# Inverse square roots: ten VectorE operations replaced by one elementwise power on GpSimd

## The chip, the cores and the metric

The kernel runs on one core of a Trainium2 chip. The metric is device time in microseconds (us), the median of several runs. The core has five engines that work side by side and meet only at semaphores: TensorE (PE, matrix products, with its weight loads as PEld), VectorE (DVE), ScalarE (ACT), GpSimd (POOL) and SyncE (SP, which issues DMAs). GpSimd has done little here: it fills constants, copies a few tiles and shares one solve with VectorE.

## The reference

One decoder layer over 16 sequences of 128 tokens with 128 channels (4 heads of 32), all float32: a delta-rule attention with gates, a cross attention without softmax, a feed-forward layer with 8 experts of which the best 2 count, and a layer norm behind each. Inverse roots and roots stand in four places of it:

```python
def l2norm(x):
    return x * jax.lax.rsqrt(jnp.sum(x * x, -1, keepdims=True) + 1e-06)      # of q and k, per head

def head_stats(x):
    mean = x.mean(-1)
    var = ((x - mean[..., None]) ** 2).mean(-1)
    am = jnp.abs(x).mean(-1)
    l2 = jnp.sqrt((x * x).sum(-1))
    return jnp.stack([mean, var, am, l2], -1).mean(2)      # mean over the heads

def rmsnorm(x, w):
    return x * jax.lax.rsqrt((x * x).mean(-1, keepdims=True) + EPS) * w

x = _layernorm(x + attention(x))
x = _layernorm(x + cross_attention(x, ctx))
x = _layernorm(x + experts(x))
```

head_stats is taken of four sources (short filter, long filter, delta-rule output, v) and of their gated mixture.

## The kernel before

The 16 sequences are worked in NG = 4 groups of G = 4. Each engine has one instruction list, written out by hand in program order, and nothing reorders it; engines wait for one another by counting semaphores. The stages, in order of time:

1. Projections (to about 110 us). Per group TensorE projects four sequences (line 460), ScalarE applies SiLU (L876) and squares q and k (L882), and VectorE in `norms` sums the squares per head (L1175), adds 1e-6 (L1178), takes the inverse root of 32 numbers per partition and scales k (L1182) and k times beta (L1189). TensorE transposes these keys (`keys_transposed`, L442) only after the next group's first projection; ScalarE copies them (L902, L906), and then the products L493 run. For the last group there is no next projection to stand in between.
2. Triangular inverse (124 to 160 us). VectorE (L1430, L1432) and GpSimd (L409, L413) share it; its input and output go through DRAM. Around it VectorE makes the statistics of v (k = 3), of the short filter (k = 0) and, later, of the long filter (k = 1): `source_sums`, then `source_moments`, each on 64 numbers per partition.
3. The delta rule (174 to 226 us): a chain of small matrix products (L721, L733, L757) on TensorE. Behind it `source_moments(2, 0, G)` finishes the statistics of the delta output for group 0 (16 numbers per partition), GpSimd copies them (`stats_of`, L425), and TensorE transposes them (L576).
4. Gates, cross attention and experts (235 us to the end). Group 0 first goes through the gate alone: `mixture_stats` (statistics of the mixture, 16 numbers), `gated` (rmsnorm, 16 numbers), `x1_norm` (layer norm, 4 numbers per partition). Then `step(g)` for g = 1, 2, 3 lays three groups over one another: the gate of group g, the cross attention and first experts of p = g - 1, the last experts of q = g - 2. VectorE's order in a step is: add(q, 5), rotate_queries(p), decay_scores(p), source_logits(g), add(q, 6), x2_norm(p), add(q, 7), source_weights(g), route_max(p), mixture(g), choose(p), finish(q), mixture_stats(g), start_sum(p), add(p, 0), add(p, 1), rotate_keys(g), add(p, 2), gated(g), add(p, 3), x1_norm(g), add(p, 4). TensorE's order is fixed in the same way: x1t(p), queries, scores, attend(p), the rest of q's experts, x2t(p), route(p), then experts of p, with st2_transposed(g), output_gate(g), output_z(g), ont(g) and wo(g) among them. A last stretch has the remaining experts of group 3 and its final layer norm.

`rsqrt` (L1140 to L1144) is a guess on the bits and three Newton rounds of three operations. Each operation ends with `own`, which makes VectorE wait for its own result. `layernorm` (x1_norm, x2_norm, finish), `norms`, `head_moments` and `gated` call it. In `head_moments` one more operation ahead (L1257, a floor of 1e-30) and one behind (L1259, times the sum of squares) turn the inverse root into a root.

```python
own(dve.tensor_scalar(y.bitcast(I32), a.bitcast(I32), -0.5, RSQRT_GUESS, ALU.mult, ALU.add))
for i in range(3):
    own(dve.tensor_tensor(out=t, in0=y, in1=y, op=ALU.mult))
    own(dve.scalar_tensor_tensor(out=t, in0=t, scalar=-0.5, in1=a, op0=ALU.mult, op1=ALU.mult))
    own(dve.scalar_tensor_tensor(out=y, in0=t, scalar=1.5, in1=y, op0=ALU.add, op1=ALU.mult))
```

## Time and profile before

| | before |
|---|---|
| median of 3 runs | 512.89 us (512.64 to 513.82) |
| span of the profiled execution, first to last instruction | 510.6 us |
| TensorE busy | 401.5 us (79%), 2952 products |
| VectorE busy | 323.2 us (63%), 1050 instructions |
| ScalarE busy | 159.2 us (31%) |
| GpSimd busy | 39.3 us (8%), 77 instructions |
| mean granted TensorE clock | 0.843 of full speed |

The profiled execution has no device time of its own beside the span; the median of the runs is 2.3 us above the span. Busy time is a sum over stages with different limits, so the table alone does not say what a shorter VectorE is worth. TensorE's clock has two levels, full (1.00, 2.4 GHz) and half (0.50, 1.2 GHz).

### The profile page before, as it was taken

The page shows a single profiled execution, that of the slowest core. Times are in us where ns is not written, and L with a number is a line of the kernel's source. Part 1 is how long each engine was busy: PE and PEld are TensorE (multiplying, and loading weights), DVE is VectorE, ACT ScalarE, POOL GpSimd, SP SyncE. Part 2 cuts the span into 40 slices and gives each one's busy share as a digit, 9 for nine tenths or more (in the row PEclk, how much of TensorE's full clock was granted, in tenths as well). Part 3 has the DMA queues.
Part 4 walks back from the last instruction along what each step waited for, and adds up shares of the span by engine and source line. Part 5 has one row for each costly group of instructions (what it writes and reads, how often), then busy time and mean ns, then how long its engine had stood idle before and what let it go on. Part 6 is the DMA issues. An engine that isn't in the chain of part 4 may idle for free.

```text
span 510.6 us, 8321 instructions
## 1 busy us (share of the span) xinstructions
PE 401.5 (79%) x2952; PEld 293.4 (57%) x2952; DVE 323.2 (63%) x1050; ACT 159.2 (31%) x267; POOL 39.3 (8%) x77
## 2 busy tenths in 40 slices
PE   1979999788973699984245689897998979887992
PEld 0647677467962699971023355565656546564672
DVE  2043464677999823368763576676897588777635
ACT  1252523512345211142021124422433244413430
POOL 7000000002980000000000000000000000000000
PEclk9989999997997555575555969999899989999997
DMA  7460201039653900000000000000020000000000
GB/s 246 105 186 1 42 0 22 1 75 296 166 145 88 119 3 3 3 2 0 1 1 27 15 21 1 0 22 0 2 62 2 21 0 21 0 0 1 22 2 21
DMA packets 48305, 22.23 MB, mean 44 GB/s; under 512 B 17768, under 2 KB 47632, under 8 KB 48016
## 3 DMA queue, kind: packets, MB, share of 16 engines
q1 hardware_dynamic: 31760, 13.40, 10.9%
q10 hardware_dynamic: 16512, 8.39, 6.0%
q8 instruction: 21, 0.34, 0.3%
q14 instruction: 12, 0.10, 0.1%
HBM read 18.64 MB, written 3.15 MB: 43 GB/s over the span
## 4 chain that ended last, share of the span: by engine, by line
PE 49%; DVE 31%; issue 9%; DMA 5%; ACT 3%; SPq 2%; DVEq 0%; ACTq 0%; POOL 0%
PE bank L460 9%; PE bank L493 5%; PE bank L691 5%; PE bank L699 5%; PE bank L721 5%; PE bank L733 4%; PE bank L442 4%; DVE prod L1430 3%; DVE inv L1432 3%; DVE as_t L1410 2%; DVE as_t L1232 2%; DVE nt L1143 2%; DVE nt L1142 2%; DVE as_t L1223 2%; DVE sm L1144 2%
## 5 line engine op out<-in xcount | busy, mean ns | idle before, releaser
L699 PEld LDWEIGHTS bank<-w_sb,as_t 128*128 128x128 f32 x512 | 61.0, 194 | 23.0 <-issue 18.8
L699 PE MATMUL bank<-w_sb,as_t 128*128 128x128 f32 x512 | 63.9, 280 | 5.0 <-ACT as_t L1002 5.0
L1002 ACT ACTIVATE as_t<-bank,cb 128x512 f32<-128x512 f32 x64 | 43.4, 687 | 76.0 <-PE bank L691 60.8
L691 PE MATMUL bank<-as_t,w_sb 128*128 128x512 f32 x128 | 66.5, 648 | 0.0
L1410 DVE SCALAR_TENSOR_TENSOR as_t<-bank,as_t 128x128 f32<-128x128 f32 x128 | 36.0, 344 | 23.4 <-PE bank L699 21.1
L460 PE MATMUL bank<-wtap,xc_pad 128*128 128x384 f32 x128 | 47.0, 514 | 3.8 <-DVE wtap L1157 3.8
L721 PE MATMUL bank<-vb,early 32*32 32x32 f32 x512 | 29.9, 236 | 11.7 <-DMA early<-inverses 11.7
L442 PE MATMUL bank<-ident,as_t 128*128 128x128 f32 (+1 forms) x64 | 12.1, 319 | 33.8 <-DVE as_t L1232 15.7
L1201 DVE TENSOR_TENSOR as_t<-bank,masks 128x512 f32 (+1 forms) x32 | 21.3, 690 | 26.7 <-PE bank L493 26.7
L460 PEld LDWEIGHTS bank<-wtap,xc_pad 128*128 128x128 f32 x128 | 25.0, 202 | 20.3 <-issue 4.3
L721 PEld LDWEIGHTS bank<-vb,early 32*32 32x32 f32 x512 | 28.2, 151 | 13.1 <-issue 12.3
L691 PEld LDWEIGHTS bank<-as_t,w_sb 128*128 128x128 f32 x128 | 24.1, 207 | 20.2 <-issue 18.8
L493 PE MATMUL bank<-early 128*128 128x256 f32 x128 | 31.1, 399 | 2.3 <-ACT early L906 2.3
L442 PEld LDWEIGHTS bank<-ident,as_t 128*128 128x128 f32 (+1 forms) x64 | 7.4, 145 | 42.0 <-DVE as_t L1232 17.3
L493 PEld LDWEIGHTS bank<-early 128*128 128x128 f32 x128 | 25.0, 200 | 5.9 <-ACT early L906 2.5
L442 PE MATMUL bank<-ident,early 128*128 128x128 f32 x96 | 15.8, 295 | 14.8 <-POOL ident L380 7.0
L1447 DVE TENSOR_TENSOR vb<-vb,bank 32x512 f32<-32x512 f32 x12 | 8.2, 686 | 27.0 <-PE bank L733 27.0
L1057 ACT ACTIVATE early<-bank 32x512 f32<-32x512 f32 x16 | 9.4, 588 | 44.3 <-PE bank L721 44.3
L733 PE MATMUL bank<-early,as_t 32*32 32x32 f32 (+2 forms) x384 | 22.7, 239 | 0.0
L442 PEld LDWEIGHTS bank<-ident,early 128*128 128x128 f32 x96 | 11.3, 150 | 18.7 <-POOL ident L380 7.0
L733 PEld LDWEIGHTS bank<-early,as_t 32*32 32x32 f32 (+2 forms) x384 | 21.3, 153 | 0.5
L876 ACT ACTIVATE early<-bank 128x384 f32<-128x384 f32 x16 | 7.9, 491 | 36.4 <-PE bank L462 36.1
(221 smaller groups left out, 647.5 us busy)
## 6 DMA issues: line engine op xcount, KB each, us to landing
toep<-taps_long ACTq DMA_DIRECT2D x8, 1024.0 KB, 7.0
toep<-x SPq DMA_DIRECT2D x8, 256.0 KB, 2.8
early<-x SPq DMA_DIRECT2D x4, 256.0 KB, 4.6
w_sb<-w SPq DMA_DIRECT2D x1, 1024.0 KB
w_sb<-w SPq DMA_DIRECT2D x2, 512.0 KB
blocks<-as_t SPq DMA_DIRECT2D x16, 64.0 KB, 2.0
early<-blocks SPq DMA_DIRECT2D x1, 1024.0 KB, 4.9
toep<-ctx_in SPq DMA_DIRECT2D x4, 256.0 KB, 3.4
```

Of the source, the lines that this page charges most:

```text
L442: last = pe.transpose(ps[dst][0:rows, b * L:(b + 1) * L], source[:, b, :], ident[:, :])
L460: pe.matmul(pr[:, 0:NQKV], xc_pad[:, b, first:first + L], wtap[:, k, :], start=(k == 0), stop=(k == TAPS - 1))
L493: last = pe.matmul(ps[4 + h][:, (b % 2) * 2 * L:(b % 2 + 1) * 2 * L], kh_c[:, h, b, :], kq_c[:, b, :, :].rearrange("p k t -> p (k t)"), st ...
L691: pe.matmul(ps[4 + half][:, :], w1_sb[:, e, half * 128:half * 128 + 128], x2_c.rearrange("p b t -> p (b t)"), start=True, stop=True).then_ ...
L699: last = pe.matmul(bank(6 + e % 2)[:, b, :], hid[:, e % 2, half, b * L:(b + 1) * L], w2_sb[:, e, half, :], start=(half == 0), stop=(half = ...
L721: last = pe.matmul(ps[6 + at % 2][rows, r * DH:(r + 1) * DH], inv_t[rows, GP * g + r, :], vb[rows, GP * g + r, :], start=True, stop=True)
L733: last = pe.matmul(ps[4 + m % 2][rows, r * DH:(r + 1) * DH], as_t[0:CH * n, GP * g + r, 0, rows], u[0:CH * n, GP * g + r, :], start=True, ...
L1002: act.activation(hid[:, e % 2, half, :], ps[4 + half][:, :], ACT.Relu, bias=c_of("b1", 2 * e + half)).then_inc(s["hid_ready"], 1)
L1201: dve.tensor_tensor(out=rows_of[:, bass.ds(g * G + 2 * r, 2), h, :], in0=bank(4 + h, 2), in1=mid(masks[:, :, :].rearrange("p k t -> p (k t ...
L1410: last = dve.scalar_tensor_tensor(out=acc[:, b, :], in0=bank(6 + e % 2)[:, b, :], scalar=score[:, b, e:e + 1], in1=acc[:, b, :], op0=ALU.m ...
L1430: own(dve.tensor_tensor(out=p, in0=blk[:, :, j, j + 1:].unsqueeze(2).broadcast_to([128, 2, m, n]), in1=wide(inv[:, :, 0:m, j], n), op=ALU. ...
L1432: own(dve.tensor_tensor(out=inv[:, :, 0:m, j + 1:], in0=inv[:, :, 0:m, j + 1:], in1=p, op=ALU.subtract))
```

## The change

Every call of `rsqrt` is taken out of VectorE. GpSimd gets a tile `exponents` (64 columns of -0.5, 64 of 0.5) and, for each root, one `tensor_tensor` with the operation `pow`: inverse root for q/k norms, gated rmsnorm and layer norms, root itself for the statistics (so L1257 and L1259 go too). For each of seven kinds there are two semaphores: VectorE raises `<kind>_squares` when the input stands, and waits for `<kind>_roots`. In `head_moments` the signal goes out ahead of the three other moment operations, which VectorE does meanwhile; in the other places VectorE waits at once. GpSimd's list of roots is written in VectorE's order; its loop over the statistics copies is unrolled and split into `source_stats` and `value_stats`, so that the copies stand between the roots.

```diff
+            def root(kind, count, y, a, n, which=0):
+
+                pool.wait_ge(s[kind + "_squares"], count)
+                pool.tensor_tensor(out=y, in0=a, in1=exponents[:, which, 0:n], op=ALU.pow
+                                   ).then_inc(s[kind + "_roots"], 1)
...
             with pool.Fori(0, NG) as g:
                 pool.wait_ge(s["silu_ready"], (g + 1) * G)
                 pool.tensor_copy(src[:, bass.ds(g * G, G), 3, :], qkv_g[:, :, 2 * D:3 * D]).then_inc(s["v_kept"], 1)
+                root("qk", g + 1, rn_g[:, :, :].rearrange("p b h -> p (b h)"),
+                     ss_g[:, :, :].rearrange("p b h -> p (b h)"), G * 2 * H)
+            root("source", 1, sm2[:, :], sumq[:, :], NP, 1)
...
+            for g in range(NG + 1):
+                if g:
+                    root("x2", g, sm2[:, 0:G], sm1[:, 0:G], G)
+                if g >= 2:
+                    root("fin", g - 1, sm2[:, 0:G], sm1[:, 0:G], G)
+                if g == NG:
+                    root("fin", g, sm2[:, 0:G], sm1[:, 0:G], G)
+                    continue
+                root("mixed", g + 1, sm2[:, 0:GP], sumq[:, 0:GP], GP, 1)
+                if g == 0:
+                    root("source", 5, sm2[:, GP:NP], sumq[:, GP:NP], NP - GP, 1)
+                    pool.wait_ge(s["stats_ready"], 5)
+                if g < NG - 1:
+                    source_stats(g + 1)
+                root("gated", g + 1, sm2[:, 0:GP], ogr.rearrange("p b h -> p (b h)"), GP)
+                if g < NG - 1:
+                    value_stats(g + 1)
+                root("x1", g + 1, sm2[:, 0:G], sm1[:, 0:G], G)
...
+            def rooted(kind, count, squares):
+
+                squares.then_inc(s[kind + "_squares"], 1)
+                dve.wait_ge(s[kind + "_roots"], count)
...
-            def head_moments(to, n, first=0):
+            def head_moments(to, n, kind, count, first=0):
 
                 mine = slice(first * H, (first + n) * H)
+                dve.sem_inc(s[kind + "_squares"], 1)
                 own(dve.tensor_tensor(out=sm1[:, mine], in0=sumx[:, mine], in1=sumx[:, mine], op=ALU.mult))
                 own(dve.scalar_tensor_tensor(out=sm1[:, mine], in0=sumq[:, mine], scalar=float(DH),
                                              in1=sm1[:, mine], op0=ALU.mult, op1=ALU.subtract))
-                dve.tensor_reduce(out=to(1), in_=sm1[:, mine].rearrange("p (n h) -> p n h", h=H),
-                                  axis=AX.X, op=ALU.add)
-                own(dve.tensor_scalar(sm2[:, mine], sumq[:, mine], 1e-30, None, ALU.max))
-                rsqrt(nt2[:, mine], sm2[:, mine], n * H)
-                own(dve.tensor_tensor(out=sm2[:, mine], in0=sumq[:, mine], in1=nt2[:, mine], op=ALU.mult))
+                own(dve.tensor_reduce(out=to(1), in_=sm1[:, mine].rearrange("p (n h) -> p n h", h=H),
+                                      axis=AX.X, op=ALU.add))
+                dve.wait_ge(s[kind + "_roots"], count)
                 own(dve.tensor_reduce(out=to(3), in_=sm2[:, mine].rearrange("p (n h) -> p n h", h=H),
                                       axis=AX.X, op=ALU.add))
```

On VectorE, at the last layer norm of the program, there stood before (as_t is the tile that holds the rows and their mean and variance, sm the variance and its inverse root, nt a scratch tile):

```order
L1227 BN_AGGR as_t<-as_t 128x2 x4
L1229 TENSOR_SCALAR sm<-as_t 128x4
L1140 TENSOR_SCALAR sm<-sm 128x4
L1142 TENSOR_TENSOR nt<-sm 128x4
L1143 SCALAR_TENSOR_TENSOR nt<-nt,sm 128x4
L1144 SCALAR_TENSOR_TENSOR sm<-nt,sm 128x4
...
L1232 TENSOR_SCALAR as_t<-as_t,sm 128x128 x4
```

and now:

```order
L1253 BN_STATS as_t<-as_t 128x6 x4
L1257 BN_AGGR as_t<-as_t 128x2 x4
L1259 TENSOR_SCALAR sm<-as_t 128x4
L1261 TENSOR_SCALAR as_t<-as_t,sm 128x128 x4
```

The ten operations are gone; the wait for GpSimd stands between the last two rows. On GpSimd, behind the solve, there stood two fills and then the copies of the statistics in a loop:

```order
L418 MEMSET as_t 128x128
L419 MEMSET as_t 128x128
L425 COPY as_t<-st_all 128x4x16
L427 COPY as_t<-st_all 128x4x4
L432 UNCONDITIONAL_BRANCH
```

and now, from the same two fills to the roots of step 1 (the rows of L401 are the powers):

```order
L433 MEMSET as_t 128x128
L434 MEMSET as_t 128x128
L401 TENSOR_TENSOR sm<-sumq,exponents 128x16
L442 COPY as_t<-st_all 128x4x16
L447 COPY as_t<-st_all 128x4x4
L401 TENSOR_TENSOR sm<-sumq,exponents 128x16
L401 TENSOR_TENSOR sm<-sumq,exponents 128x48
L442 COPY as_t<-st_all 128x4x16
L401 TENSOR_TENSOR sm<-as_t,exponents 128x16
L447 COPY as_t<-st_all 128x4x4
L401 TENSOR_TENSOR sm<-sm,exponents 128x4 x2
L401 TENSOR_TENSOR sm<-sumq,exponents 128x16
```

The powers have 4, 16 or 48 columns there (32 in the projections, 64 around the solve), and each copy now stands behind the power ahead of it.

## Rows read from the trace of the kernel before

**Rows 1.** The page, part 2: TensorE's granted clock in 40 slices

```profile
PEclk9989999997997555575555969999899989999997
```

**Rows 2.** The page, part 4: the chain that ended last, by engine

```profile
PE 49%; DVE 31%; issue 9%; DMA 5%; ACT 3%; SPq 2%; DVEq 0%; ACTq 0%; POOL 0%
```

**Rows 3.** Timeline, x1 norm of group 2: start us, us, engine, line, operation, out<-in

```profile
391.94 0.17 DVE L1140 TENSOR_SCALAR sm<-sm 128x4 int32<-128x4 int32 x1
...
393.92 1.12 DVE L1232 TENSOR_SCALAR as_t<-as_t,sm 128x128 f32<-128x128 f32 x4
```

**Rows 4.** Timeline, moments of the delta output, group 0, and what follows

```profile
231.16 0.17 DVE L1252 TENSOR_TENSOR sm<-sumx 128x16 f32<-128x16 f32 x1
...
234.16 0.17 DVE L1260 TENSOR_REDUCE st_all<-sm 128x4 f32<-128x16 f32 x1
234.37 0.17 DVE L1284 TENSOR_TENSOR st_all<-st_all,stat_scale 128x16 f32<-128x16 f32 x1
...
234.73 0.24 POOL L425 COPY as_t<-st_all 128x64 f32<-128x64 f32 x1 [7.46 <-issue]
...
235.02 1.03 PE L576 MATMUL bank<-ident,as_t 128*32 128x128 f32 x4 [6.62 <-POOL as_t L425]
```

**Rows 5.** Timeline, moments of the mixture, group 0

```profile
253.77 0.17 DVE L1252 TENSOR_TENSOR sm<-sumx 128x16 f32<-128x16 f32 x1
...
256.77 0.17 DVE L1260 TENSOR_REDUCE as_t<-sm 128x4 f32<-128x16 f32 x1
```

**Rows 6.** Timeline, gated rmsnorm, group 0

```profile
264.69 0.17 DVE L1140 TENSOR_SCALAR sm<-as_t 128x16 int32<-128x16 int32 x1
...
266.78 0.18 DVE L1342 TENSOR_TENSOR as_t<-sm,as_t 128x16 f32<-128x16 f32 x1
```

**Rows 7.** Timeline, q/k norm of the last group

```profile
94.32 0.18 DVE L1140 TENSOR_SCALAR rn_g<-ss_g 128x32 int32<-128x32 int32 x1
...
96.09 0.60 ACT L895 ACTIVATE src<-bank 128x512 f32<-128x512 f32 x1 [0.35 <-PE bank L473]
...
96.56 0.69 DVE L1182 TENSOR_TENSOR early<-early,rn_g 128x512 f32<-128x512 f32 x1
...
97.31 0.33 PE L442 MATMUL bank<-ident,early 128*128 128x128 f32 x1 [1.34 <-DVE early L1182]
```

**Rows 8.** Timeline, GpSimd in the solve: smallest and largest two-input operation

```profile
124.06 0.29 POOL L409 TENSOR_TENSOR wtap<-early,inv 128x40 f32<-128x40 f32 x1 [31.53 <-DMA early<-blocks]
...
137.56 0.88 POOL L409 TENSOR_TENSOR wtap<-early,inv 128x220 f32<-128x220 f32 x1
```

**Rows 9.** Timeline, where VectorE waits behind a root

```profile
124.00 0.23 DVE L1430 TENSOR_TENSOR prod<-early,inv 128x62 f32<-128x62 f32 x1 [2.06 <-DMA early<-blocks]
...
224.36 0.69 DVE L1465 TENSOR_TENSOR src<-bank,rq 128x512 f32<-128x512 f32 x1 [2.31 <-PE bank L442]
...
314.92 0.69 DVE L1403 TENSOR_TENSOR as_t<-bank,as_t 128x512 f32<-128x512 f32 x1 [3.02 <-PE bank L684]
```

**Rows 10.** TensorE's waits, 277 to 452 us: total, times, longest

```profile
PE bank L442 <- DVE as_t L1232: 14.2, 6, 5.5
...
PE bank L442 <- DVE as_t L1344: 1.9, 3, 0.7
```

**Rows 11.** Timeline, two such waits behind 452 us

```profile
452.43 0.65 PE L442 MATMUL bank<-ident,as_t 128*128 128x128 f32 x4 [0.42 <-DVE as_t L1232]
...
466.77 0.66 PE L442 MATMUL bank<-ident,as_t 128*128 128x128 f32 x4 [1.06 <-DVE as_t L1232]
```

**Rows 12.** Timeline, first-layer products of one expert, twice in step 3

```profile
415.10 3.56 PE L691 MATMUL bank<-as_t,w_sb 128*128 128x512 f32 x4
...
421.41 1.88 PE L691 MATMUL bank<-as_t,w_sb 128*128 128x512 f32 x4
```

**Rows 13.** Windows: length, busy PE, PEld, DVE, ACT, POOL (x instructions), clock, DMA share, GB/s

```profile
386.00:390.00 4.00, 2.58 (x15) 1.80 (x15) 2.24 (x7) 1.35 (x3) 0.00 (x0) 1.00 0.00 0
...
416.00:418.00 2.00, 2.00 (x4) 0.58 (x2) 1.71 (x6) 0.78 (x2) 0.00 (x0) 0.50 0.00 0
```

More of the change, by code:

```diff
@@ L27 @@
 FLOOR = 0.02
-RSQRT_GUESS = float(0x5F3759DF)
 WB = {}
@@ L245, in decoder_kernel @@
                  "hid_ready y_ps sum_started y_added fin_ready").split()
+        names += [kind + end for kind in ("qk", "source", "mixed", "gated", "x1", "x2", "fin")
+                  for end in ("_squares", "_roots")]
         s = {n: sem(n) for n in names}
@@ L416, in _ @@
             pool.sem_inc(s["solved"], 1)
+            root("source", 2, sm2[:, :], sumq[:, :], NP, 1)
+            root("source", 3, sm2[:, :], sumq[:, :], NP, 1)
             pool.wait_ge(s["o_ps"], NG)
@@ L420, in _, with source_stats, value_stats @@
             pool.wait_ge(pool_step, 15)
-            def stats_of(g):
+            root("source", 4, sm2[:, 0:GP], sumq[:, 0:GP], GP, 1)
+            def source_stats(g):
                 pool.wait_ge(s["st_ps"], g + credit["st_ps"])
-                pool.tensor_copy(st[:, :, 0:16], st_all[:, bass.ds(g * G, G), :]).then_inc(s["st_ready"], 1)
+                pool.tensor_copy(st[:, :, 0:16], st_all[:, g * G:(g + 1) * G, :]).then_inc(s["st_ready"], 1)
+            def value_stats(g):
                 pool.wait_ge(s["st2_ps"], g + credit["st2_ps"])
-                pool.tensor_copy(st2[:, :, 4:8], st_all[:, bass.ds(g * G, G), 12:16]).then_inc(s["st2v_ready"], 1)
+                pool.tensor_copy(st2[:, :, 4:8], st_all[:, g * G:(g + 1) * G, 12:16]).then_inc(s["st2v_ready"], 1)
             pool.wait_ge(s["stats_ready"], 4)
-            stats_of(0)
-            pool.wait_ge(s["stats_ready"], 5)
-            with pool.Fori(1, NG) as g:
-                stats_of(g)
+            source_stats(0)
+            value_stats(0)
+            for g in range(NG + 1):
[16 more added lines that the diff above has]
+                root("x1", g + 1, sm2[:, 0:G], sm1[:, 0:G], G)
         @block.tensor
@@ L1135, in own @@
                 dve.wait_ge(dve_step, base[0] + base[1])
-            def rsqrt(y, a, n):
-                t = nt1[:, 0:n]
-                own(dve.tensor_scalar(y.bitcast(I32), a.bitcast(I32), -0.5, RSQRT_GUESS, ALU.mult, ALU.add))
-                for i in range(3):
-                    own(dve.tensor_tensor(out=t, in0=y, in1=y, op=ALU.mult))
-                    own(dve.scalar_tensor_tensor(out=t, in0=t, scalar=-0.5, in1=a, op0=ALU.mult, op1=ALU.mult))
-                    own(dve.scalar_tensor_tensor(out=y, in0=t, scalar=1.5, in1=y, op0=ALU.add, op1=ALU.mult))
+            def rooted(kind, count, squares):
+                squares.then_inc(s[kind + "_squares"], 1)
+                dve.wait_ge(s[kind + "_roots"], count)
             def wide(a, m):
@@ L1177, in norms @@
                                       axis=AX.X, op=ALU.add))
-                own(dve.tensor_scalar(ss_g[:, :, :], ss_g[:, :, :], 1e-6, None, ALU.add))
-                rsqrt(rn_g[:, :, :].rearrange("p b h -> p (b h)"), ss_g[:, :, :].rearrange("p b h -> p (b h)"),
-                      G * 2 * H)
+                rooted("qk", g + 1, dve.tensor_scalar(ss_g[:, :, :], ss_g[:, :, :], 1e-6, None, ALU.add))
                 dve.wait_ge(s["kh_ps"], g + credit["kh_ps"])
@@ L1206, in _ @@
             norms(0)
-            PROJ_STEPS = 13
+            PROJ_STEPS = 2
             start = base[1]
@@ L1218, in _, with layernorm @@
                 mask_products(NG - 1, r)
-            def layernorm(y, dst, done):
+            def layernorm(y, dst, kind, count):
                 for b in range(G):
@@ L1228, in layernorm @@
                 own(last)
-                own(dve.tensor_scalar(sm1[:, 0:G], mv[:, :, 1], EPS, None, ALU.add))
-                rsqrt(sm2[:, 0:G], sm1[:, 0:G], G)
+                rooted(kind, count, dve.tensor_scalar(sm1[:, 0:G], mv[:, :, 1], EPS, None, ALU.add))
                 for b in range(G):
@@ L1233, in layernorm @@
                                              ALU.subtract, ALU.mult)
-                last.then_inc(s[done], 1)
+                last.then_inc(s[kind + "_ready"], 1)
             def head_sums(xs, squares, to, n):
@@ L1339, in gated @@
                                       in1=wide(sm1[:, 0:G], H), op=ALU.mult))
-                own(dve.tensor_scalar(ogr, ogr, 1.0 / DH, EPS, ALU.mult, ALU.add))
-                rsqrt(sm2[:, 0:G * H], ogr.rearrange("p b h -> p (b h)"), G * H)
+                rooted("gated", g + 1, dve.tensor_scalar(ogr, ogr, 1.0 / DH, EPS, ALU.mult, ALU.add))
                 own(dve.tensor_tensor(out=ogr, in0=sm2[:, 0:G * H].rearrange("p (b h) -> p b h", b=G),
@@ L1479, in _ @@
             mixture_stats(0)
-            source_moments(2, G, B)
+            source_moments(2, G, B, 5)
             gated(0)
@@ L1514, in _ @@
             step(1, False)
-            MIX_STEPS = 101
+            MIX_STEPS = 46
             start = base[1]
```

28 lines of the change are left out of this document (15 added, 13 removed).

## The prediction, made before the changed kernel ran

> **What bounds the kernel now.** I read the chain of waits first, by engine. TensorE has 49% of it and VectorE 31% [rows 2]. A small GpSimd operation has nothing to fear from GpSimd's own work, which is 8% of the span. A share of a chain is not a price, though: where VectorE is on the chain, TensorE may be only a step behind. So I went to the timeline around each group of roots and asked each time what the next instruction on TensorE had waited for. There are three kinds of places.
>
> In the first, TensorE stands idle until VectorE is done, and the whole root is on the path. These are the moments of the delta output for group 0 (VectorE, GpSimd's copy, TensorE's transpose follow one another within 0.9 us) [rows 4], the moments of the mixture of group 0 [rows 5], its gated rmsnorm [rows 6], its x1 norm and the x2 norm of group 0, and the last norm of the program, behind which no product stands. The two norms of group 0 show as the two waits of about 5.5 us in TensorE's list of waits [rows 10].
>
> In the second, in the steps, TensorE is nearly full and waits only briefly for a norm or the gated product. From 277 to 452 us it waited six times and 14.2 us for a norm; without the two long ones (5.5 each, 11.1 together by the timeline) 3.16 us are left for four waits. It waited three times and 1.9 us for the gated product [rows 10], and then 0.42 and 1.06 us for two more norms [rows 11]. A root may shrink by more than that there; what TensorE gets back is the wait, and then its own queue binds. This is where the chain of waits misleads: it gives almost all of 348 to 386 us to VectorE.
>
> In the third, VectorE waits for something else behind the root, so nothing is gained: the statistics of v (then 2.06 us of waiting for a DMA), of the long filter (then 2.31 us of waiting for TensorE), of the mixture in step 1 (then 3.02 us) [rows 9]. The statistics of the short filter stand under the DMA of the inverses, and those of groups 1 to 3 of the delta output under TensorE's output gate. The q/k norms of groups 0 to 2 stand under TensorE's next projection.
>
> **What one root costs.** Removed: on 4 columns, from the start of the guess to the start of the operation that uses the root, 393.92 - 391.94 = 1.98 us [rows 3]; on 16 columns in the gated product 266.78 - 264.69 = 2.09 us [rows 6]; on 32 columns 96.56 - 94.32 = 2.24 us [rows 7]. In the moments the floor and the last product go too, and the signal is given ahead of the three other operations: from the first of them to the sum that needs the root it is 234.16 - 231.16 = 3.00 us [rows 4], and 256.77 - 253.77 = 3.00 us [rows 5].
>
> Added: a hand-off to GpSimd, the power, and a hand-off back. VectorE's operation ended at 234.37 + 0.17 = 234.54 and GpSimd's copy began at 234.73: 0.19 us. The copy ended at 234.97 and TensorE began at 235.02: 0.05 us [rows 4]. Together 0.24 us.
>
> No row shows a power. An ordinary two-input operation on GpSimd takes 0.29 us on 40 columns and 0.88 us on 220 [rows 8], so 0.59 / 180 = 3.3 ns a column and 0.16 us fixed. Lower end: a power costs no more than that, 0.17 us on 4 columns. Upper end: ten whole GpSimd operations, as VectorE needs ten: 10 x (0.16 + 0.013) = 1.7 us on 4 columns, 10 x 0.21 = 2.1 us on 16. I take the value between: one instruction with ten passes over each column, 33 ns a column and 0.16 us fixed. That is 0.29 us on 4 columns, 0.69 on 16, 1.22 on 32, 2.3 on 64. With the hand-offs a root takes 0.53, 0.93 and 1.46 us on 4, 16 and 32 columns. It is the row's own speed times the work that the removed code had to do; a built-in power should not need more passes than the guess and its rounds.
>
> The Trainium skill speaks against the change: GPSIMD Engine Reference, section "Engine selection", gives elementwise work to VectorE because GpSimd is about twice as slow for two inputs. Read operation for operation that would make a root on 4 columns twice 1.98 us, and every root on the path would lose about 2 us, ten such places some 20 us. The trace does not decide it, since what is exchanged is ten instructions for one.
>
> **The sum.** On the path in full:
> - moments of the delta output and of the mixture, group 0: 3.00 - 0.93 = 2.07 each, 4.14 us. The three operations that run beside the power take about 0.7 us, so they do not end later than it.
> - gated product of group 0: 2.09 - 0.93 = 1.16 us.
> - x1 and x2 norm of group 0 and the last norm: 3 x (1.98 - 0.53) = 4.35 us.
> - q/k norm of the last group: 2.24 - 1.46 = 0.78 us, but the keys' transpose also waits for ScalarE's copy, which ended at 96.09 + 0.60 = 96.69, while it began at 97.31 [rows 7]. With a hand-off of 0.04, 0.58 us. Behind it stand DMAs that move with it.
>
> Capped by TensorE's waits in the steps: 3.16 + 0.42 + 1.06 = 4.64 us for six norms (the longest is 1.21, below the 1.45 that each root gives), and 1.9 us for three gated products (the root gives 1.16 each). Together 6.5 us.
>
> Sum: 4.14 + 1.16 + 4.35 + 0.58 + 6.5 = 16.7 us.
>
> Then the clock. The granted clock has dips at about 357, 408 and, less deep, 470 us [rows 1]: right behind the x2 norm TensorE works at 0.50 from 416 to 418 us [rows 13], and one expert's first layer takes 3.56 us that takes 1.88 a little later [rows 12], 1.7 us more. Ahead of it TensorE had a row of gaps, of which the wait for the x2 norm is the largest. From 386 to 390 us it was busy 2.58 of 4 us and the clock stayed at 1.00 [rows 13], so gaps of the size that would be left do not always cost it. If all three dips go, that is 3 x 1.7 = 5 us; if none does, nothing. I take half, 2.5 us. The long half-clock stretches at 166 to 217 and 230 to 281 us stay.
>
> All in all 19.2 us. Against the profiled execution's span this is 510.6 - 19.2 = 491.4 us; the median of the runs lies 2.3 us above that span, so 512.89 - 19.2 = **493.7 us**.
>
> **What the moved copies do.** GpSimd takes its instructions in order, so each copy of statistics now waits behind the power ahead of it. The copy that TensorE needs at once, of group 0, comes behind the power that its own input needs anyway. The others are needed half a step later. A late power would hold VectorE, with all of its later list behind it, and through it TensorE. The solve on GpSimd now stands behind the power for the statistics of v, 64 columns; its cover is the 2.06 us of DMA wait plus the time that VectorE no longer spends, about 5 us against 2.3.
>
> **The rivals.**
> 1. *The power is slower, but not by much*, say 85 ns a column. A root is then 0.74, 1.76 and 3.12 us. The three full norms give 3.7 us, the capped ones still 4.64, the two moments 2 x 1.24 = 2.5, four gated products 0.33 each, 1.3, and the last q/k norm costs 0.9. 11.3 us gained, no clock: 501.6 us. For it: nothing says that ten passes suffice. Against: 85 ns is 26 times the ordinary column.
> 2. *Slower than before: the power is a long routine per column.* Place: the q/k norms (32 columns) and gated products (16), where VectorE waits with nothing beside it. At 200 ns a column a root is 1.2, 3.6 and 6.8 us. Norms: 3 x 0.78 + 3.5 = 5.8 us gained; moments 1.2 lost; gated products 4 x 1.5 = 6 lost; the last q/k norm 4.6 lost, and the other three as much each less TensorE's cover, 0 to 14. That is 6 to 20 us, about 524 us. It decides from about 150 ns a column on. For it: the 16 partitions that must be served at once may be served by a loop. Against: ordinary operations show no such thing.
> 3. *TensorE's queue gives nothing back*: a wait that VectorE no longer causes is taken over by ScalarE or by the next exchange, in the steps and in the path of group 0, and the powers are near the upper end. Gain under 1 us: 512.4 us. Against it: in group 0 TensorE is idle for whole microseconds, and ScalarE has been waiting too.
> 4. *The first power loads its code.* The first two-input operation on GpSimd took 0.29 us at once [rows 8], with nothing ahead of it. A load would fall into the q/k norm of group 0 and push TensorE once by what goes beyond its cover. By the row the price is nothing; I allow a few microseconds, 497 us. The Trainium skill (GPSIMD Engine Reference, section "Instruction dispatch") states about 6 us for the first call of a freshly loaded kernel; by that figure the sum would be at most 6 us smaller. No row here shows such a load.
>
> **How the numbers follow.** Forecast 0.58, rival 1 0.14, rival 2 0.18, rival 3 0.06, rival 4 0.04. Forecast alone: 489 us (power at the ordinary price, all dips gone) to 498 (no dip gone, hand-offs twice as long). For 8 in 10 the range must take in rival 1 and its slower neighbours and leave most of rival 2 outside: 488.5 to 510. A measurement of this kernel tells changes from about 0.2%, 1 us, on. Faster: forecast, rivals 1 and 4, 0.76. Same: rival 3, 0.06. Slower: rival 2, 0.18.
>
> **What would show it.** In the profile of the changed kernel: the power on 4 columns near 0.3 us, on 16 near 0.7, on 32 near 1.2; between VectorE's operation ahead of it and the one behind it 0.5 and 0.9 us; VectorE's busy time down by some 50 us; the waits of 5.5 us for the norms of group 0 near 4; TensorE's short waits for norms and gated products in the steps gone, and a step some 2 to 4 us shorter rather than the 7 that VectorE saves; the dips behind the x2 norms gone or shorter. The prediction is wrong in its main term if the power on 16 columns takes over 2 us, and in its reading of the steps if they shorten by much more than TensorE's waits, or if TensorE keeps waiting for norms although VectorE has become shorter.

## The result and the profile after

The changed kernel takes 529.39 us (median of 4 runs, 528.83 to 530.82), the kernel before 512.76 us on the same chip (4 runs, 512.59 to 513.82). The ratio is 1.0331, interval 1.0304 to 1.0357: 3.3% slower, 16.6 us. I had forecast 493.7 us and 488.5 to 510. The profiled execution took 528.99 us with a span of 527.3 (before 510.6) at a mean granted clock of 0.835 (before 0.843). Executions more than 1.5% above the fastest of the same kernel are left out of every time and ratio below.

The page of the changed kernel: the clock row of part 2 [rows 1 has the one of before] and the chain of part 4 [rows 2].

```profile
PEclk9989999967998555557555586999999989989998
```
```profile
PE 39%; DVE 23%; POOL 16%; issue 15%; ACT 3%; DMA 1%; DVEq 0%; SPq 0%; POOLq 0%; ACTq 0%
POOL sm L401 13%; PE bank L496 7%; PE bank L735 5%; PE bank L727 5%; PE bank L757 3%; PE bank L769 3%; DVE inv L1459 3%; DVE prod L1457 3%; POOL rn_g L401 3%; PE bank L478 3%; PE bank L529 2%; DMA cb<-cbundle 1%; DVE as_t L1261 1%; PE bank L653 1%; DVE as_t L1437 1%
```

GpSimd had none of the chain and now has 16% of it; the powers are line 401. The page's part 1 has VectorE at 269.0 us (51%) and GpSimd at 138.7 (26%). VectorE lost its work, as the change says, and the time went up. The groups of GpSimd by line and form give the reason in six lines (out<-in and shapes, then times it ran | busy us, mean ns of one | idle before it):

```profile
L401 POOL TENSOR_TENSOR sm<-sumq,exponents 128x64 f32<-128x64 f32 x3 | 31.7, 10550 | 77.6 <-DVEq L1281 77.6
L401 POOL TENSOR_TENSOR rn_g<-ss_g,exponents 128x32 f32<-128x32 f32 x4 | 21.7, 5437 | 8.9 <-DVE ss_g L1210 8.9
L401 POOL TENSOR_TENSOR sm<-sumq,exponents 128x16 f32<-128x16 f32 x5 | 14.5, 2901 | 46.4 <-DVEq L1281 46.4
L401 POOL TENSOR_TENSOR sm<-sm,exponents 128x4 f32<-128x4 f32 x12 | 12.1, 1008 | 153.0 <-DVE sm L1259 153.0
L401 POOL TENSOR_TENSOR sm<-as_t,exponents 128x16 f32<-128x16 f32 x4 | 11.6, 2902 | 32.8 <-DVE as_t L1368 32.8
L401 POOL TENSOR_TENSOR sm<-sumq,exponents 128x48 f32<-128x48 f32 x1 | 8.0, 8020 | 0.4 <-DVEq L1281 0.4
```

A power takes (10.55 - 1.008) / (64 - 4) = 0.159 us a column and 0.37 us fixed; the line meets the other sizes too: 16 columns 2.91 (measured 2.90), 32 columns 5.46 (5.44), 48 columns 8.00 (8.02). I had assumed 0.033 a column and 0.16 fixed.

Now the places, in the timeline after. The x1 norm of group 0 shows what the change does well [rows 3 show the ten operations of such a norm]:

```profile
294.18 0.17 DVE L1259 TENSOR_SCALAR sm<-as_t 128x4 f32<-128x4 f32 x1
295.47 1.11 DVE L1261 TENSOR_SCALAR as_t<-as_t,sm 128x128 f32<-128x128 f32 x4 [1.12 <-POOL sm L401]
```

1.12 us pass between the two, where 2.0 passed before: 0.09 us to GpSimd, 1.01 for the power, 0.03 back. The norm gains 0.9 us. The last q/k norm, 32 columns, is [rows 7] again, VectorE, GpSimd and TensorE in turn:

```profile
98.00 0.18 DVE L1210 TENSOR_SCALAR ss_g<-ss_g 128x32 f32<-128x32 f32 x1
...
98.26 5.43 POOL L401 TENSOR_TENSOR rn_g<-ss_g,exponents 128x32 f32<-128x32 f32 x1 [1.84 <-DVE ss_g L1210]
...
103.73 0.69 DVE L1212 TENSOR_TENSOR early<-early,rn_g 128x512 f32<-128x512 f32 x1 [5.55 <-POOL rn_g L401]
...
104.47 1.06 PE L478 MATMUL bank<-ident,early 128*128 128x128 f32 x4 [4.61 <-DVE early L1212]
```

VectorE stands still for 5.55 us in place of 2.24 us of work, and TensorE waits 4.61 us where it waited 1.34. The group ends 7.2 us later than before: 104.47 - 97.31.

The statistics of v, 64 columns, were for me a root that costs nothing, since VectorE waited for a DMA behind it [first row of rows 9]. After:

```profile
124.51 10.55 POOL L401 TENSOR_TENSOR sm<-sumq,exponents 128x64 f32<-128x64 f32 x1 [20.82 <-DVEq L1281]
135.03 0.25 POOL L422 TENSOR_TENSOR wtap<-early,inv 128x40 f32<-128x40 f32 x1
...
135.17 0.22 DVE L1288 TENSOR_REDUCE st_all<-sm 128x16 f32<-128x64 f32 x1 [7.74 <-POOL sm L401]
135.43 0.28 DVE L1312 TENSOR_TENSOR st_all<-st_all,stat_scale 128x64 f32<-128x64 f32 x1
135.86 0.27 DVE L1457 TENSOR_TENSOR prod<-early,inv 128x62 f32<-128x62 f32 x1 [0.15 <-DVE st_all L1312]
```

Both halves of the solve now stand behind the power, GpSimd's at once and VectorE's by three more operations. TensorE was 8.9 us late at 110 us, the solve starts 11.9 us late (135.86 - 124.00): 2.9 us lost here. The DMA that VectorE waited for before is no longer what ends the wait. (Its landing is not fixed either: in the run with the cheap last norms below, where nothing is changed so early, VectorE starts its part of the solve at 127.78 behind that DMA.) The statistics of the long filter and the gated product of group 0:

```profile
231.80 0.22 DVE L1285 TENSOR_REDUCE st_all<-sm 128x16 f32<-128x64 f32 x1
241.43 0.22 DVE L1288 TENSOR_REDUCE st_all<-sm 128x16 f32<-128x64 f32 x1 [9.41 <-POOL sm L401]
...
244.82 2.12 PE L478 MATMUL bank<-ident,inv 128*128 128x128 f32 x8 [3.95 <-ACT inv L1100]
...
282.70 0.20 DVE L1288 TENSOR_REDUCE st_all<-sm 128x12 f32<-128x48 f32 x1 [7.30 <-POOL sm L401]
...
287.15 0.18 DVE L1369 TENSOR_TENSOR as_t<-sm,as_t 128x16 f32<-128x16 f32 x1 [3.02 <-POOL sm L401]
...
288.11 0.69 PE L478 MATMUL bank<-ident,as_t 128*128 128x128 f32 x2 [7.10 <-DVE as_t L1371]
```

VectorE stands still for 9.41, 7.30 and 3.02 us for its statistics and the gated root, and TensorE then for 7.10 us, where it waited 4.20 before.

To add this up, take the start of the same TensorE instruction in both traces and subtract. TensorE is late by 3.9 us ahead of the last q/k norm, 7.2 behind it, 8.9 at 110 us of the time before; 12.5 at 177; 14.4 at 220; 18.0 at 235; 20.4 at 268 (gated product); 19.1 at 295; 17.6 at 498. So all of the loss lies before the first layer norm, and from there the changed kernel gains 2.8 us. The growth between 97 and 110 us, 1.8 us, is the clock: right behind TensorE's 4.61 us of standing it is granted about half, near the lower of its two levels, 1.2 GHz. The first row below is the start of that stretch. The second is all of it, up to the first product of line 577 (window rows of after: start:end, length, busy PE, ..., clock):

```profile
104.40:112.00 7.60, 5.30 (x16) 4.11 (x17) 4.57 (x10) 4.75 (x6) 0.00 (x0) 0.51 0.22 35
104.47:118.78 14.31, 12.08 (x41) 9.52 (x41) 8.65 (x15) 4.75 (x6) 0.00 (x0) 0.64 0.12 18
```

Before, the same 41 products ran at 0.86; they kept TensorE busy for 10.11 us where it is 12.08 now, and it was idle for 2.4 us then and 2.2 now:

```profile
97.31:109.86 12.55, 10.11 (x41) 8.04 (x41) 8.65 (x15) 4.75 (x6) 0.00 (x0) 0.86 0.13 21
```

### The profile page after: what moved, and what is told of

Its sections match the earlier page's. It is cut to its first block, busy times and chain, and to the rows that moved or that the text cites. A ratio compares the mean times of both kernels' runs of the same rounds, so it can differ in the third digit from the quotient of the medians.

```text
span 527.3 us, 7911 instructions
## 1 busy us (share of the span) xinstructions
PE 405.7 (77%) x2952; PEld 297.4 (56%) x2952; DVE 269.0 (51%) x742; ACT 158.6 (30%) x267; POOL 138.7 (26%) x108
## 4 chain that ended last, share of the span: by engine, by line
PE 39%; DVE 23%; POOL 16%; issue 15%; ACT 3%; DMA 1%; DVEq 0%; SPq 0%; POOLq 0%; ACTq 0%
POOL sm L401 13%; PE bank L496 7%; PE bank L735 5%; PE bank L727 5%; PE bank L757 3%; PE bank L769 3%; DVE inv L1459 3%; DVE prod L1457 3%; POOL rn_g L401 3%; PE bank L478 3%; PE bank L529 2%; DMA cb<-cbundle 1%; DVE as_t L1261 1%; PE bank L653 1%; DVE as_t L1437 1%
## 5 line engine op out<-in xcount | busy, mean ns | idle before, releaser
L401 POOL TENSOR_TENSOR sm<-sumq,exponents 128x16 f32<-128x16 f32 (+2 forms) x9 | 54.2, 6019 | 124.4 <-DVEq L1281 124.4
L735 PE MATMUL bank<-w_sb,as_t 128*128 128x128 f32 x512 | 65.0, 283 | 5.0 <-ACT as_t L1038 5.0
L401 POOL TENSOR_TENSOR sm<-sm,exponents 128x4 f32<-128x4 f32 x12 | 12.1, 1008 | 153.0 <-DVE sm L1259 153.0
L478 PE MATMUL bank<-ident,as_t 128*128 128x128 f32 (+1 forms) x64 | 11.9, 316 | 33.5 <-DVE as_t L1371 11.5
L529 PE MATMUL bank<-early 128*128 128x256 f32 x128 | 32.4, 412 | 2.2 <-ACT early L942 2.2
L478 PE MATMUL bank<-ident,early 128*128 128x128 f32 x96 | 17.4, 313 | 20.6 <-POOL ident L382 7.1
L401 POOL TENSOR_TENSOR rn_g<-ss_g,exponents 128x32 f32<-128x32 f32 x4 | 21.7, 5437 | 8.9 <-DVE ss_g L1210 8.9
```

The source lines that it names most:

```text
L401: pool.tensor_tensor(out=y, in0=a, in1=exponents[:, which, 0:n], op=ALU.pow).then_inc(s[kind + "_roots"], 1)
L478: last = pe.transpose(ps[dst][0:rows, b * L:(b + 1) * L], source[:, b, :], ident[:, :])
L529: last = pe.matmul(ps[4 + h][:, (b % 2) * 2 * L:(b % 2 + 1) * 2 * L], kh_c[:, h, b, :], kq_c[:, b, :, :].rearrange("p k t -> p (k t)"), st ...
L735: last = pe.matmul(bank(6 + e % 2)[:, b, :], hid[:, e % 2, half, b * L:(b + 1) * L], w2_sb[:, e, half, :], start=(half == 0), stop=(half = ...
```

## The experiments

My theory after the trace (A): the map of the path in the prediction is right, and one number in it, the price of a power, is not. With it, roots on 4 columns gain and those on 32, 48 and 64 lose, each where its cover is short. Rivals: that single gains do not arrive; that clock and order of the work, not the powers, set the difference. (Each expectation says for itself what its letters from B on stand for.) In the kernels below a tuple names the kinds of roots that are powers, and all others are the ten VectorE operations of before. Each was timed beside the kernel before, in at least three rounds unless said otherwise.

A time alone mixes waits and clock. So this table takes the same instructions of TensorE out of each profiled execution, by the starts of their first ones: from the gated product of group 0 to the transposes behind its x2 norm (268.01 to 295.08 us of the time before, with two norms in it), and the steps (295.08 to 498.08). Idle is the length of the stretch less TensorE's busy time in it. Busy time is that of the same products each time (947 or 948 of them are recorded), so it differs by the clock.

| kernel | idle, 268 to 295 | idle in the steps | busy in the steps | clock there |
|---|---|---|---|---|
| before | 12.10 | 22.10 | 180.90 | 0.95 |
| changed | 10.32 | 21.17 | 180.30 | 0.94 |
| cheap operation | 8.72 | 16.45 | 174.24 | 0.97 |
| only the norms | 10.35 | 18.26 | 179.74 | 0.94 |
| norms and moments | 10.32 | 18.56 | 175.43 | 0.97 |
| the same, repeated | 10.33 | 18.75 | 178.95 | 0.95 |
| gated product too | 10.32 | 21.04 | 180.39 | 0.94 |
| each norm power twice | 12.28 | 24.08 | 179.18 | 0.96 |
| last kind of norm, cheap | 12.10 | 21.99 | 178.86 | 0.96 |

**The cheap operation.** Every power becomes a multiplication by a constant (1e-6 for q and k, 0.01 in the moments, 0.5 elsewhere); waits, order and hand-offs stay. The inverse roots are thus left out.

```diff
-                pool.tensor_tensor(out=y, in0=a, in1=exponents[:, which, 0:n], op=ALU.pow
+                pool.tensor_tensor(out=y, in0=a, in1=exponents[:, which, 0:n], op=ALU.mult
```

> The changed kernel with every power on GpSimd replaced by a multiplication by a constant at the same place, in the same order and with the same semaphores; the roots themselves are left out. Theory A (the loss is the length of the powers, and nothing else in the move costs anything): an operation of 4, 16, 32 columns takes 0.17, 0.21, 0.27 us, with the hand-offs 0.41, 0.45, 0.51 us. On the path in full 4.6 + 1.6 + 4.7 + 0.6 us, capped by TensorE's waits 6.5 us, together 18.0 us, and 0 to 5 us from the clock: 490 to 495 us. Theory B (the exchange itself costs: the added waits, the copies behind the roots, GpSimd's solve behind a root): above 503 us although the operations are short.

487.93 us (486.82 to 489.4), ratio 0.9514 [0.9476, 0.9553]. That is 5.8 us below the forecast of 493.7, which was for a cheap power, and below the 490 to 495 expected here. The same stretch of steps, in this run and before (the window rows behind the table):

```profile
283.62:474.31 190.69, 174.24 (x948) 118.91 (x947) 121.48 (x426) 71.14 (x114) 3.83 (x19) 0.97 0.04 12
295.08:498.08 203.00, 180.90 (x948) 120.76 (x948) 146.98 (x582) 72.19 (x114) 0.63 (x3) 0.95 0.04 11
```

TensorE's idle time in the steps fell by 5.65 us, close to the 6.5 of the caps. Its busy time fell by 6.66 us, which is the clock; with 1.0 us between 268 and 295 this is three times the 2.5 of the clock term. Of the two dips to 0.8 behind 350 us in [rows 1] its clock row keeps one (each digit is 12.1 us of this shorter span), which is what that term was about:

```profile
PEclk9989999987998655557555869999999899999999
```

This settles where the prediction failed: the path, the hand-offs and the caps were right enough, the price was not. The clock term, too small, does not explain a slower kernel.

**Only the norms.** The twelve layer-norm roots on 4 columns (the expectation counts thirteen by mistake; its sum takes nine).

```diff
+POWERS = ('x1', 'x2', 'fin')
+SOURCES = ()
```

> Only the thirteen layer norm roots (4 columns) go to GpSimd as powers; q/k norms, statistics and gated products have VectorE's ten operations again. Theory A: a power of 4 columns with its hand-offs takes 1.12 us in the changed kernel against 2.01 us before, 0.89 us gained a root; three in full 2.7 us, six in the steps up to TensorE's waits 3.8 us: 506.3 us, 505 to 508. Theory B: 510 us or more, since the waits are there as well.

507.3 us (505.47 to 510.79), ratio 0.9894 [0.9832, 0.9956]. The time is near A's, but by itself it does not shut out the 510 of theory B. The table does: TensorE is idle 1.75 us less between 268 and 295, for two norms of 0.89, and 3.84 us less in the steps, where A had 3.8.

**Norms and the two kinds of 16-column moments** (of the mixture, and of the delta output for group 0).

```diff
-POWERS = ('x1', 'x2', 'fin')
-SOURCES = ()
+POWERS = ('x1', 'x2', 'fin', 'mixed')
+SOURCES = (4,)
```

> As the run with the layer norms alone, and also the moments of the mixture and of the delta output of group 0 (16 columns, signal given ahead of three other operations) as powers. Theory A: from the first moment operation to the sum that needs the root it is 2.49 us in the changed kernel against 3.00 before, 0.5 us twice: 505.3 us, 1 us below the run with the norms alone. Theory B: not below it.

500.71 us (499.73 to 504.0), ratio 0.9772 [0.9719, 0.9824], 4.6 us below what was expected. I ran the same kernel again in five rounds, with this expectation:

> The kernel with the layer norms, the moments of the mixture and those of the delta output of group 0 as powers (4 and 16 columns), once more: 500.7 us by its first runs, by the terms worked out ahead of them 505.3. If the first runs were lucky with TensorE's clock, it comes out nearer to 505; if not, 500 to 501.5.

502.95 us (501.07 to 506.86), ratio 0.9797 [0.9764, 0.983]. So it is 2.0 to 2.3% faster than before. TensorE's waits say why (group, what it waited for: us, times, longest). From 290 to 466 us of the first of the two runs:

```profile
PE bank L488 <- DVE as_t L1287: 5.4, 4, 4.7
...
PE bank L488 <- DVE as_t L1410: 2.2, 3, 0.9
```

and of before, from 294 to 468 us:

```profile
PE bank L442 <- DVE as_t L1232: 10.2, 7, 5.5
```

Without the long one of each, the short waits for norms fell from 4.7 to 0.7 us: the caps of [rows 10, 11] came back almost in full. The two moments of group 0 give 0.5 us each, as A has it: TensorE's idle time falls from 6.95 to 6.42 us between 177 and 235 us of the time before, and from 13.38 to 12.87 between 235 and 257. The rest is the clock, which also makes the two runs differ. The same stretch of steps in the first run

```profile
292.41:486.40 193.99, 175.43 (x947) 118.92 (x947) 126.30 (x456) 71.92 (x114) 18.52 (x16) 0.97 0.04 12
```

and in the repeated run:

```profile
292.80:490.50 197.70, 178.95 (x948) 120.94 (x948) 126.41 (x456) 71.94 (x114) 18.52 (x16) 0.95 0.04 11
```

The same kernel is idle for 18.6 and 18.8 us there, and busy for 175.4 and 179.0.

**The five source statistics back on VectorE**, all else as powers.

```diff
+POWERS = ('qk', 'mixed', 'gated', 'x1', 'x2', 'fin')
+SOURCES = ()
```

> The changed kernel with the five source statistics (64, 64, 64, 16 and 48 columns) back on VectorE; all else as changed. Theory A: the stages in which these powers hold VectorE or GpSimd grew by 2.9 (start of the solve), 2.4 (short filter), 4.3 (long filter), 1.9 (48 columns) us and the 16 column one gained 0.6: about 11 us come back, 518.5 us. Theory B: under 4 us come back, over 525 us.

515.93 us (513.32 to 518.85, eight of ten executions), ratio 1.0058 [1.0025, 1.009]. The 64- and 48-column roots cost some 13.5 us of the 16.6, more than the 11 of A.

**The q/k roots back on VectorE**, all else as powers.

```diff
+POWERS = ('mixed', 'gated', 'x1', 'x2', 'fin')
+SOURCES = (1, 2, 3, 4, 5)
```

> The changed kernel with the four q/k norm roots (32 columns, powers of 5.4 us) back on VectorE; all else as changed. Theory A: the whole growth of the projections, 8.7 us at the last product of that stage less the 0.5 us that other runs show there, comes back and nothing behind it changes: 521.2 us. Theory B (the early groups' roots stand under TensorE's next projection, as the prediction has it, and only the last group's counts): 3.5 us come back, 526 us.

519.57 us (515.6 to 522.76), ratio 1.0117 [1.0047, 1.0188]: 9.8 us less than with them, near A. The four q/k groups cost in the way that rival 2 had said: in the changed kernel the first three made TensorE 3.9 us late, by what goes beyond its next projection, the last one 3.3 us in full, and the clock behind it 1.8 us.

**Only the three 64-column roots as powers**, in the kernel before.

```diff
+POWERS = ()
+SOURCES = (1, 2, 3)
```

> The kernel before with nothing moved but the three roots of 64 columns (statistics of v, of the short and of the long filter) as powers on GpSimd. The prediction counted them as hidden: 513 us. Theory A: a power of 64 columns takes 10.55 us and starts beside the third sum; the statistics of v then end 2.9 us behind the DMA for which the solve waited, those of the short filter hold VectorE until after TensorE needs it (about 2 us), those of the long filter hold it about 4 us: 8.5 to 9 us lost, 522 us.

532.38 us (529.62 to 532.88), ratio 1.0352 [1.0321, 1.0383]: 18.6 us, twice what A gave. The trace splits it. At 110 us of the time before, ahead of the roots, TensorE is 1.0 us late, at 257 us 10.7: 9.7 us are the roots and what follows from them, near A. It is 6.3 at 362 and 18.2 at 412, where no root was changed, and 19.9 at the end. The same stretch of TensorE's list, in this run

```profile
368.25:430.53 62.28, 54.62 (x252) 38.60 (x253) 41.05 (x165) 18.30 (x29) 0.20 (x1) 0.84 0.06 18
```

and before:

```profile
362.00:412.37 50.37, 45.28 (x252) 30.75 (x252) 39.49 (x160) 18.64 (x29) 0.20 (x1) 1.00 0.08 22
```

The clock is 0.84 where it was 1.00, TensorE is busy 9.3 us longer with the same products and idle 2.6 us more. All four runs lie close together (529.6 to 532.9), so this is no accident of one. Why a program that only comes some 6 us later there gets less clock I can't say; it stays open.

**The gated product's root too**, on top of the norms and moments.

```diff
-POWERS = ('x1', 'x2', 'fin', 'mixed')
+POWERS = ('x1', 'x2', 'fin', 'mixed', 'gated')
```

> The kernel of the run with the layer norms and the moments of the mixture (500.7 us), and the gated product's root (16 columns, VectorE waits at once) as a power too. In the changed kernel it is 3.01 us from the operation ahead of the root to the one behind it, before 2.13 us: 0.88 us lost a root. Theory A: TensorE waits for each of the four: 3.5 us lost, 504.2 us. Theory C (TensorE's queue sets the end of a step, so only group 0's counts): 501.6 us.

509.85 us (508.14 to 510.94), ratio 0.9932 [0.9907, 0.9958]: 6.9 us more than the repeated run without it. Directly each such root is 3.01 - 2.13 = 0.88 us longer, four times 3.5 us, and TensorE's waits for the gated product over the steps went from 2.2 to

```profile
PE bank L488 <- DVE as_t L1410: 4.4, 3, 1.5
```

that is 2.2 for three of them. The traces place what goes beyond. Between the two profiled executions lie 6.3 us: 1.5 are there at 36 us already, ahead of any change; 0.9 is the gated product of group 0; in the steps TensorE is idle 2.3 us longer, which is the other three, and busy 1.4 us longer, which is the clock. So the price of the root is 3.2 us, near A.

**Each norm power done twice**, in the kernel with norms and moments.

```diff
+                if kind in ("x1", "x2", "fin"):
+                    pool.tensor_tensor(out=exponents[:, 1, 60:60 + n], in0=a, in1=exponents[:, which, 0:n], op=ALU.pow)
```

> The same kernel as that of 500.7 us, but each layer norm's power on GpSimd is done twice, the first into a spare place: a root takes 2.13 us in place of 1.12 us. Theory A (each layer norm is on the path, and what the move gave in the steps was the wait of TensorE): three in full 3.0 us, six in the steps 1.0 us each, 9 us lost, 509.8 us. Theory C (in the steps VectorE has room to spare, so that only the three norms outside count): 503.7 us.

513.38 us (511.75 to 515.85), ratio 0.9992 [0.9974, 1.0009]: 10.4 us above the repeated run, for twelve powers of 1.01 us. The two profiled executions are 12.0 us apart, and 2.7 of them are there at 177 us, ahead of the first norm, where no power explains them. Behind it TensorE is idle 1.95 us longer between 268 and 295 and 5.33 us longer in the steps, and the last norm ends 1.0 us later by its root: 8.3 us, against the 9 of A and the 3 of C. With 2.1 us a norm is as long as it was: nine of the twelve are on the path, as the prediction's list had it.

**The last kind of norm for almost nothing**: in the kernel before, only the norms after the experts go to GpSimd, as a multiplication. Their inverse root is left out.

```diff
+POWERS = ('fin',)
...
-                pool.tensor_tensor(out=y, in0=a, in1=exponents[:, which, 0:n], op=ALU.pow
+                pool.tensor_tensor(out=y, in0=a, in1=exponents[:, which, 0:n], op=ALU.mult
```

> The kernel before with one kind of root alone moved, that of the last of each group's layer norms (behind the experts), and there a multiplication by a constant in place of the power, so the root is left out for these. A root falls from 2.01 to about 0.45 us. Theory D (the prediction's: in the steps TensorE's full queue sets the time and only a wait of TensorE can be won; nothing but the very last norm counts): 1.6 us gained, 511.5 us against 513.1. Theory E (the chain of waits: VectorE is on it in steps 2 and 3 where two more of these norms stand): 3 x 1.6 = 4.7 us gained, 508.4 us.

509.6 us (507.57 to 512.34), ratio 0.9914 [0.9892, 0.9936]: 4.2 us gained, 3.3 to 5.5 by the interval, which has E's 4.7 in it and not D's 1.6. The trace says otherwise about the cause. In the steps TensorE's idle time is what it was, 21.99 for 22.10 us, so no wait was won there, as D has it. What fell is the busy time of the same products, by 2.0 us: the clock. The tail gives its part in full, 1.7 us: VectorE's last group follows the hand-off by 0.31 us.

```profile
505.91 0.17 DVE L1284 TENSOR_SCALAR sm<-as_t 128x4 f32<-128x4 f32 x1
506.39 1.11 DVE L1287 TENSOR_SCALAR as_t<-as_t,sm 128x128 f32<-128x128 f32 x4 [0.31 <-POOL sm L411]
```

From 450 to 498 us of the time before the grant is 1.00 here and 0.96 in the kernel before and in the one with each norm power twice. The prediction's list had nothing for a norm that ends no wait of TensorE, and here such norms came with 2 us of clock. That they are what brings it is not shown: the kernel with the gated product's root as a power has short norms too, and 0.96 there.

**The price by itself.** Seven operations on GpSimd in a stretch in which it has nothing to do.

```diff
+            for parts, n, x, op in ((128, 1, price, ALU.pow), (128, 8, price, ALU.pow), (128, 32, price, ALU.pow),
+                                    (128, 32, exponents, ALU.pow), (64, 32, price, ALU.pow),
+                                    (16, 32, price, ALU.pow), (128, 32, price, ALU.mult)):
...
+                pool.tensor_tensor(out=price[0:parts, 1, 0:n], in0=x[0:parts, row, 0:n],
+                                   in1=exponents[0:parts, 0, 0:n], op=op).then_inc(s["exponents_set"], 1)
```

> The kernel with the norms and the two 16-column moments as powers, and seven more operations on GpSimd between its last copy of v (about 92.5 us) and the solve, which measure the price of a power by itself; their results are used by nothing. In order: powers on 128 partitions of 1, 8 and 32 columns with input 3.0; 32 columns with input 0.5; 32 columns with input 3.0 on 64 and on 16 partitions; a multiplication of 32 columns. The line through the powers of the changed kernel (1.01 us at 4 columns, 10.55 at 64: 0.37 us and 159 ns a column) says 0.53, 1.64 and 5.46 us for the first three. Theory A (a fixed routine per column, whatever the data and however many partitions): the other three powers 5.46 us each too. Theory B (the cost lies with the elements, spread unevenly over the cores): on 64 partitions 2.9 and on 16 partitions 1.0 us. Theory C (the routine depends on the data): 0.5 takes another time than 3.0. The multiplication: 0.27 us by the ordinary line. The seven take some 24 us, so the solve starts on time and the kernel takes 501 to 504 us.

501.15 us (one run). The groups of line 429; the first holds the power on 128 partitions with input 3.0 (5.43 us, the timeline row at the end) and the multiplication:

```profile
L429 POOL TENSOR_TENSOR price<-price,exponents 128x32 f32<-128x32 f32 x2 | 5.7, 2842 | 0.2
L429 POOL TENSOR_TENSOR price<-exponents 128x32 f32<-128x32 f32 x1 | 5.4, 5430 | 0.1
L429 POOL TENSOR_TENSOR price<-price,exponents 64x32 f32<-64x32 f32 x1 | 5.4, 5422 | 0.1
L429 POOL TENSOR_TENSOR price<-price,exponents 16x32 f32<-16x32 f32 x1 | 5.4, 5418 | 0.1
...
L429 POOL TENSOR_TENSOR price<-price,exponents 128x8 f32<-128x8 f32 x1 | 1.7, 1657 | 0.1
...
L429 POOL TENSOR_TENSOR price<-price,exponents 128x1 f32<-128x1 f32 x1 | 0.6, 565 | 0.1
```
```profile
94.52 5.43 POOL L429 TENSOR_TENSOR price<-price,exponents 128x32 f32<-128x32 f32 x1
```

Input 3.0 or 0.5, and 128, 64 or 16 partitions: 5.42 to 5.43 us. The multiplication takes 2 x 2.842 - 5.43 = 0.25 us, a twentieth. Theory A of this run holds: a fixed time per column, for the inputs tried.

## Why the prediction was wrong

**The step that failed** is the price in "What one root costs": "one instruction with ten passes over each column, 33 ns a column". It is 159 ns, 48 times the 3.3 ns of the ordinary column. That was outside my bounds as well: the upper end for 16 columns was 2.1 us, the measured value is 2.90. On 4 columns the power stayed inside them, 1.01 against 1.7 us, since they were built from a fixed part of ten instructions and the measured one grows with the columns. The argument that a built-in power should not need more passes than guess and rounds had no row behind it. Two instructions that both read two tiles share the form of the record, not the work, and [rows 8] could bound only the fixed part.

**The crossover.** With the hand-offs a root is 0.12 + 0.37 + 0.159 n us on n columns, against 2.0 to 2.2 us on VectorE whatever n from 4 to 32: equal at about 10. Twelve of the 29 powers have 4 columns and gain 0.89 us each; five are moments on 16 columns, with three operations beside the power, and gain a little (3.00 to 2.49 us for the mixture of group 0); the other twelve lose. The change put one remedy on 4 and on 64 columns alike.

**The third kind of place.** "VectorE waits for something else behind the root, so nothing is gained" was right and beside the point: a place where nothing can be gained can still lose, by cover. I worked the cover out for one of them (5 us against 2.3, the statistics of v) and for none of the others; with a power of 10.55 us the three places of 64 columns lost 2.9, 1.9 and 3.6 us. The last two are the lateness from 177 to 220 and from 220 to 235 us, so the moments of the delta output's group 0 are in the last one. The first three q/k norms, also counted as covered, lost 3.9 us.

**Rival 2** was the right mechanism, and had its place at the q/k norms right. Its own sum gave about 524 us at 200 ns a column. At 159 ns the same sum gains about 6.6 us with the norms and loses 3.4 with the gated products, 3.3 with the last q/k norm and 0 to 10 with the other three: 0 to 10 us lost. The measured loss is 16.6, because the 48- and 64-column roots were left out of the sum; without the source powers the kernel is 0.6% slower than before. So the threshold "from about 150 ns" stood too high for this change as a whole, and 0.18 was too little for the case in which no row had the price.

**Rival 1** fell with the price. **Rival 3** fell: the gains on 4 and 16 columns arrive in the time. **Rival 4** fell in the first power: it starts 0.09 us behind VectorE's operation, like the others, and takes 5.45 us against a mean of 5.44 for its kind, so no load shows in it. The Trainium skill, GPSIMD Engine Reference, section "Instruction dispatch", has about 6 us for such a load; this trace does not show it.

**What held.** The norms of group 0 as full gains, and the caps: the short waits for norms in the steps fell by 4.0 us where 4.64 were allowed for, and with the cheap operation TensorE's idle time in the steps by 5.65 where 6.5 were. The two hand-offs of a norm take 0.12 us together, where I took 0.24. With the cheap operation the sum of waits held too. The profiled execution gained 25.5 us: 4.9 for the two moments, 1.8 for the gated product, 3.4 and 1.7 for the three norms, 0.5 for the last q/k norm and 5.65 in the steps, 17.9 us together where the sum had 16.7. VectorE's busy time fell to 269.0 us in the changed kernel, by 54 where some 50 were expected.

**A second term was mis-sized**, the clock, 2.5 us for the dips in the steps. It had the right sign, but the rest of the 25.5 us, 7.6, is the clock, so that 487.93 was measured for the 493.7 that the forecast gives to a cheap power, just outside its range. It does not move the kernel to the slower side. The changed kernel itself won only 0.6 us of it in the steps (180.30 busy for 180.90).

**The rule that I had weighed**, of the Trainium skill, GPSIMD Engine Reference, section "Engine selection", gives elementwise addition, multiplication and maximum to VectorE, since GpSimd takes about twice as long for two inputs. It does not speak of a power, and read for one its factor is far off: one power on 32 columns takes 5.44 us where the whole VectorE root takes 2.24, and one on 4 columns takes half of the root. That the rule read operation for operation gave some 20 us of loss and 16.6 were measured is luck: it charged the norms 2 us each, and they gained 0.89.

## What to carry to other kernels

Before an operation that no row shows is put in many places, run it once by itself at two sizes; until then keep the range as wide as the unknown price makes it, with every place in the sum, those that "cost nothing" first. Replacing many short instructions by one pays where the instructions are short because the tile is small (here up to some 10 columns) and the other engine's price is per column. A wait that hides a step hides it only up to its own length: write that length beside each place counted as free.

## What the runs showed that I had not expected

- GpSimd's power on fp32 costs 0.16 us for each column and about 0.4 us fixed, on 16 as on 128 partitions, for inputs 3.0 and 0.5, for exponent -0.5 (2.902 us on 16 columns) and 0.5 (2.901).
- One wait of 4.61 us on TensorE was followed by 7.6 us at a grant of 0.51 (14.3 us at 0.64), where the same 41 products had 0.86 behind a wait of 1.34 us.
- A stretch of the program with nothing changed in it ran at 1.00 or at 0.84 of the clock, in two kernels that differ only ahead of it, and took 50.4 or 62.3 us. A difference of a few microseconds between two variants of this kernel is not yet a difference of their instructions; the start of each TensorE instruction compared between the traces shows where it arose, and idle and busy time over the same instructions tell waits from clock.
